# Attention with projections in halves, weighing of two slots in odd ones, and a split of the eight PSUM banks into four, three and one

## What is computed

```python
qh = (q @ Wq + bq).reshape(B, LQ, HEADS, D_K).transpose(0, 2, 1, 3)
kh = (k @ Wk + bk).reshape(B, LKV, HEADS, D_K).transpose(0, 2, 1, 3)
vh = (v @ Wv + bv).reshape(B, LKV, HEADS, D_K).transpose(0, 2, 1, 3)
scores = jnp.einsum('bhqd,bhkd->bhqk', qh, kh) * scale
attn = jax.nn.softmax(scores, axis=-1)
out = jnp.einsum('bhqk,bhkd->bhqd', attn, vh)
```

## Time and profile before

| | us |
|---|---|
| median of 3 runs | 1433.04 |
| lowest, highest | 1431.14, 1434.31 |
| the profiled execution, its own time | 1427.45 |
| its span, first to last instruction | 1425.7 |
| slots 0 to 510 within it | 65.87 to 959.19 |

### The profile page before, as it was taken

One profiled execution on the slowest core, in us unless ns is written; L12 is line 12 of the kernel. 1 busy time (PEld: TensorE's weight loads), 2 busy tenths in 40 slices (PEclk: granted clock), 3 DMA queues, 4 the chain that ended last, 5 costly groups with the idle time before them and its releaser, 6 DMA issues.

```text
span 1425.7 us, 32607 instructions
## 1 busy us (share of the span) xinstructions
PE 1372.8 (96%) x13186; PEld 757.5 (53%) x13186; DVE 1070.9 (75%) x2114; ACT 962.1 (67%) x1931; POOL 287.7 (20%) x321
## 2 busy tenths in 40 slices
PE   7799999999999999999999999998989999989998
PEld 4344444444444444444444545456547999856666
DVE  4787877778787778777778888835876768767757
ACT  5377777777777777777777666672896664448731
POOL 3353121222212222121222100000003100001210
PEclk9899999999999999999999999999999999999999
DMA  5865453335445335544424632002401320347000
GB/s 172 191 160 151 119 134 93 90 92 135 115 122 121 73 90 128 131 113 106 112 68 102 192 83 46 2 1 60 119 24 59 111 68 0 92 117 151 2 1 30
DMA packets 98790, 134.53 MB, mean 94 GB/s; under 512 B 11024, under 2 KB 74128, under 8 KB 92688
## 3 DMA queue, kind: packets, MB, share of 16 engines
q1 hardware_dynamic: 98640, 132.45, 36.8%
HBM read 94.15 MB, written 38.27 MB: 93 GB/s over the span
## 4 chain that ended last, share of the span: by engine, by line
PE 83%; DVE 7%; ACT 7%; issue 2%; DMA 1%; POOL 0%; SPq 0%; DVEq 0%; ACTq 0%; POOLq 0%
PE psum L546 19%; PE psum L566 18%; PE psum L527 7%; PE psum L592 4%; PE psum L632 4%; PE psum L2147 4%; PE psum L2121 3%; PE psum L1241 2%; PE psum L2866 2%; DVE peaks L693 1%; ACT probs L791 1%; ACT key_f L824 1%; PE psum L2876 1%; PE psum L275 1%; PE psum L1638 1%
## 5 line engine op out<-in xcount | busy, mean ns | idle before, releaser
L693 DVE TENSOR_REDUCE peaks<-psum 128x1 f32<-128x512 f32 x1024 | 654.6, 685 | 168.7 <-PE psum L527 157.1
L791 ACT ACTIVATE probs<-psum 128x512 f32<-128x512 f32 x1024 | 555.9, 595 | 126.8 <-PE psum L546 125.0
L546 PE MATMUL psum<-queriesT,keysT 64*128 64x256 bf16 (+1 forms) x4096 | 331.9, 272 | 11.0 <-ACT probs L791 9.8
L566 PE MATMUL psum<-probs,values 128*17 128x256 f32 x4096 | 320.5, 385 | 0.0
L546 PEld LDWEIGHTS psum<-queriesT,keysT 64*128 64x128 bf16 (+1 forms) x4096 | 171.9, 94 | 219.4 <-ACT probs L791 159.3
L527 PE MATMUL psum<-keysT,queriesT 64*128 64x512 bf16 x1024 | 210.2, 379 | 7.3 <-DVE peaks L693 4.0
L566 PEld LDWEIGHTS psum<-probs,values 128*17 128x17 f32 x4096 | 68.0, 95 | 160.4 <-issue 151.3
L927 POOL CAST key_parts<-key_f 128x512 bf16<-128x512 f32 x57 | 34.9, 612 | 516.0 <-ACT key_f L824 509.7
L592 PE MATMUL psum<-ctxT,wk 128*128 128x512 f32 x128 | 75.1, 670 | 2.2 <-DVE probs L736 0.9
L527 PEld LDWEIGHTS psum<-keysT,queriesT 64*128 64x128 bf16 x1024 | 59.8, 94 | 26.1 <-DVE peaks L693 17.5
L632 PE MATMUL psum<-wv,ctxT 128*128 128x256 f32 x256 | 72.0, 407 | 0.5 <-DVE probs L724 0.4
(11 more groups left out here) (315 smaller groups left out, 1647.7 us busy)
## 6 DMA issues: line engine op xcount, KB each, us to landing
keysT<-key_parts SPq DMA_DIRECT2D x186, 256.0 KB, 5.5
key_parts<-key_parts SPq DMA_DIRECT2D x90, 256.0 KB
ctx_nat<-in_ctx_dram SPq DMA_DIRECT2D x32, 256.0 KB, 3.2
ctx_in<-in_ctx_dram SPq DMA_DIRECT2D x24, 256.0 KB, 3.1
ctx_turned<-ctxT SPq DMA_DIRECT2D x24, 256.0 KB, 6.0
ctx_T<-ctx_turned SPq DMA_DIRECT2D x12, 512.0 KB, 3.9
qk_parts<-early_weights SPq DMA_DIRECT2D x24, 128.0 KB
q_parts<-q_parts SPq DMA_DIRECT2D x20, 128.0 KB
```

What stands on the lines that cost most here:

```text
L546: made = e.matmul(ps[j][:, e2 * S:(e2 + 1) * S], self.keysT[own, plane, i % RING, kt * P:(kt + 1) * P], self.queriesT[own, plane, u % 2, g ...
L566: made = e.matmul(k.bank(SUMS)[32 * quad:32 * quad + DH + 1, 0:S], self.values[b % 2][:, kt, g * GH + j, :], self.probs[:, (SLOTS * i + p) ...
L693: e.tensor_reduce(self.peaks[:, i % 2, j * QT + qt, c:c + 1], k.ps(("max", n)), AX.X, ALU.max).then_inc(*self.peaked.up(n))
L791: e.activation(self.probs[:, t % RINGP, 2 * j * S:(2 * j + 2) * S], k.ps(("scores", t, j)), ACT.Exp).then_inc(*self.exped.up((t, j)))
```

## The change

Four things are changed together, in the first attention alone.

- **Banks**: scores rotate through four banks (0, 1, 2, 4) in place of three; maxima and jobs rotate through three (5, 6, 7) in place of four, from slot -1 on.
- **Weighing**: BLOCK is 2 in place of 1. Odd slots weigh the slots t - 3 and t - 2 together, with 16 matmuls in a row; even slots weigh nothing.
- **Halves**: the chunks of keys from the third unit on (u >= 2) are made as two jobs "fill half" of 256 rows, two slots apart. Of the values, the pieces 10 to 15 of a sequence are made as two jobs "make half" of 128 rows. Each half takes a bank and an evacuation of its own. GpSimd splits a chunk after its second half.
- **Slots of the jobs**: those that were in odd slots or shared an even one move, so that the even slots of a sequence carry about one job each (a few carry "turn shift" or "normalize" as well); "write parts" is one slot later.

```diff
-SCORES, SUMS, BLOCK = (0, 1, 2), 3, 1
+SCORES, SUMS, BLOCK = (0, 1, 2, 4), 3, 2
...
+    HALF_VALUES = {10: (-36, -28), 11: (-20, -14), 12: (-12, -6), 13: (-4, 2), 14: (4, 10), 15: (12, 14)}
...
-            at(-16 + 5 * c, "fill keys", 1, c)
+            at(-16 + 5 * c + (c in (5, 7)), "fill keys", 1, c)
...
-                at(slot + 2, "fill keys", u, c)
+                at(slot + 2, "fill half", u, c, 0)
+                at(slot + 4, "fill half", u, c, 1)
                 if c % 2:
-                    at(slot + 6, "write parts", u, c // 2)
+                    at(slot + 7, "write parts", u, c // 2)
...
-                at(SLOTS * NG * b + (8 * p - 96 if p < 12 else (-6, 0, 2, 8)[p - 12]), "make values", b, p)
+                slot = SLOTS * NG * b
+                if p in self.HALF_VALUES:
+                    for e2, after in enumerate(self.HALF_VALUES[p]):
+                        at(slot + after, "make half", b, p, e2)
+                else:
+                    at(slot - 94 + 8 * p, "make values", b, p)
...
-            choice = (7, 0, 1, 2) if t < -1 else (4, 5, 6, 7)
+            choice = (7, 0, 1, 2) if t < -1 else (5, 6, 7)
...
-            if (t - 1) % BLOCK == 0 and BLOCK + 1 <= t <= TOTAL + 1:
+            if t % BLOCK == 1 and BLOCK + 1 <= t <= TOTAL + 1:
                 i, p0 = divmod(t - BLOCK - 1, SLOTS)
                 b, g = divmod(i, NG)
                 w.wait_ge(self.exped, (t - 2, 1))
@@ -591,6 +598,20 @@
...
+                elif job == "fill half":
+                    u, c, h = a
+                    b, m = divmod(u, KD)
+                    ps = misc(t, ("keys", u, c, h), (self.key_kept, (u, c) if h else ("half", u, c)))
+                    w.wait_ge(*self.ctx_turned(b, c))
+                    e.matmul(ps[:, 0:S], self.wk[:, 0, m * P:(m + 1) * P], self.ctxT[:, c * BANK + h * S:c * BANK + (h + 1) * S],
+                             start=True, stop=True).then_inc(*self.key_made.up((u, c) if h else ("half", u, c)))
+                elif job == "make half":
+                    b, p, e2 = a
+                    ps = misc(t, ("v", b, p, e2), (self.v_kept, (b, p) if e2 else ("half", b, p)))
+                    w.wait_ge(*self.ctx_turned(b, 2 * p * P // BANK))
+                    kt = 2 * p + e2
+                    e.matmul(ps[:, 0:D], self.ctxT[:, kt * P:(kt + 1) * P], self.wv[:, 0, :], start=True, stop=True).then_inc(
+                        *self.v_made.up((b, p) if e2 else ("half", b, p)))
...
+                elif job == "fill half":
+                    u, c, h = a
+                    w.wait_ge(self.key_made, (u, c) if h else ("half", u, c))
+                    self.wait_key_f(w, (u, c))
+                    e.activation(self.key_f[:, self.turns[u, c] % 2, h * S:(h + 1) * S], k.ps(("keys", u, c, h))[:, 0:S], ACT.Identity,
+                                 bias=self.bk[:, u % KD:u % KD + 1]).then_inc(*self.key_kept.up((u, c) if h else ("half", u, c)))
+                elif job == "make half":
+                    b, p, e2 = a
+                    w.wait_ge(self.v_made, (b, p) if e2 else ("half", b, p))
+                    e.activation(self.values[b % 2][:, 2 * p + e2, :, 0:DH],
+                                 k.ps(("v", b, p, e2))[:, 0:D].rearrange("p (h d) -> p h d", h=H), ACT.Copy).then_inc(
+                        *self.v_kept.up((b, p) if e2 else ("half", b, p)))
...
+                elif job == "fill half" and a[2]:
+                    yield tuple(a[0:2])
...
-                if job == "fill keys" and not (a[0] == 0 and a[1] in self.ON_VECTOR):
-                    u, c = a
+                if job == "fill half" and a[2] or job == "fill keys" and not (a[0] == 0 and a[1] in self.ON_VECTOR):
+                    u, c = a[0:2]
```

## The result

The changed kernel takes 1467.38 us (median of 4 runs, 1464.18 to 1468.04); the kernel before, beside it, 1432.09 (1426.86 to 1434.31). The ratio is 1.0247, with an interval of 1.0215 to 1.0280: slower by about 35 us. The forecast was 1458 with a range of 1446 to 1472.

What follows compares the result with a forecast made beforehand. TensorE's own order of work was taken as the bound. +20 us for three runs of 128 slots, +1 for slots 0 to 31, +5 for 416 to 491, -1 for the last: +25, median 1433.0 to 1458, range 1446 to 1472.

Steps and rivals of the forecast that it cites:

- The deciding term: Three banks for maxima and jobs: odd slot's second maximum waits to 1.75 us, stalling pairs with a half 0.35 to 0.40.
- rival C: Double weighing: the second weighing saves nothing, 1.12 us rather than 1.02 in 255 pairs, +26 on top, 1483; chance 3%.
- rival B: Odd slot's second maximum: the bank loop binds only in part, gain and loss cancel at 1430 to 1436 us; chance 4%.
- Rival A: Odd slot's second maximum: the bank loop doesn't bind, pairs cost 3.18 us, kernel faster at 1391 to 1403; chance 8%.
- Three runs of 128 slots: The three runs from slot 32 on: pair prices summed to 682.5 us against 661.2, or +21.3, taken as +20 for upward roundings.
- first of the two maxima waits to 1.75: Pairs with a half and the shift: TensorE arrives at 1.61 us, waits for the bank until 1.75, pair 3.55.
- Slots 416 to 491: Stretch with the next part's long steps: VectorE's other work meets a shorter rotation, +1.4 to +8 us, taken as +5.
- rival D: VectorE's side work hits the short rotation everywhere, more in slots 416 to 491: +10 to +30 us, 1468 to 1488; chance 7%.
- The ends: Slots 0 to 31: +1 us (0 to +3); last slots, near ScalarE's exponentials as bound: -1 (0 to -2).
- Costs put at nothing: Halves' extra evacuations on ScalarE, GpSimd starting a chunk two slots later, SyncE writing parts one slot later: no cost.

## Why the prediction was right, and where it was off

**The deciding term held.** The loop of 0.41 + 1.29 + 0.05 = 1.75 us was read on the trace of before; 1.76 was measured. Pairs with a half, values and nothing cost 3.52, 3.59 and 2.93, for 3.55, 3.63 and 2.94. The double weighing is 0.99, for 1.02, so rival C is out, and with the full stall rival B. Waits of maxima for reductions are 85.1 us, where 60 to 90 were said. Rival A, the faster kernel, is what the old banks and the half reductions give: pairs with a half at 3.18 and 3.15 for its 3.18, 128 slots at 212.7 and 212.5 for its 211, and 1416 and 1396 us in all. Its price was about right and its condition not met, since rotation by itself doesn't hide a reader. The Trainium skill ("Perfetto Trace Analysis", section "Optimizing Tensor Performance") advises rotation through banks; these runs agree only where the time between two uses of a bank is longer than the reader takes.

**Three runs of 128 slots: +26.8 us, for +20.** I wrote 3.55 for context with "normalize" and it is 3.94, 4 times; 3.7 for "normalize" with a half and it is 4.0, 3 times; and 4.0 for the three jobs, which take 4.6. The step that failed is "first of the two maxima waits to 1.75": it followed the banks of the maxima and not that of the second job. The turned context is the second use after the even slot's first maximum and "normalize" the third, so that it comes to this maximum's bank. The timeline at such a slot of the kernel after:

```profile
134.54 0.38 PE L534 MATMUL psum<-keysT,queriesT 64*128 64x512 bf16 x2
134.85 0.42 PEld L590 LDWEIGHTS psum<-const,ctx_in 128*128 128x128 f32 x4 [0.32 <-DVE peaks L714]
...
135.70 0.52 PEld L674 LDWEIGHTS psum<-const,outT 128*128 128x128 f32 x4 [0.43 <-DVE peaks L714]
```

By its price it would be there at 0.31 + 0.59 = 0.90 and gets it at 1.16 (134.54 to 135.70), which is my own 0.41 + 0.68 + 0.05 = 1.14 for an empty pair. These eight pairs are worth 3.1 us in 128 slots, 9 in three runs. The other pairs came out up to 0.05 cheaper than I said and give back some 4, so that 21.3 before rounding became 26.8. The roundings did go upwards; that I took 20 for it moved the sum the wrong way all the same.

**Slots 416 to 491: +11 us, for +5, beyond my bound of 8.** Here rival D holds. The timeline at slot 443, where the next part's statistics (L1358 to L1362) run on VectorE:

```profile
869.36 0.69 DVE L1435 TENSOR_TENSOR x<-psum,x 128x512 f32<-128x512 f32 x1 [1.60 <-PE psum L1276]
...
871.29 0.17 DVE L1362 TENSOR_SCALAR small<-small 128x2 f32<-128x2 f32 x1
871.37 2.48 DVE L714 TENSOR_REDUCE peaks<-psum 128x1 f32<-128x512 f32 x4
...
872.10 0.09 PEld L534 LDWEIGHTS psum<-keysT,queriesT 64*128 64x128 bf16 x1 [1.75 <-DVE peaks L714]
872.11 0.39 PE L534 MATMUL psum<-keysT,queriesT 64*128 64x512 bf16 x1 [1.36 <-DVE peaks L714]
```

and the same place in the kernel before:

```profile
837.29 0.69 DVE L1400 TENSOR_TENSOR x<-psum,x 128x512 f32<-128x512 f32 x1 [1.23 <-PE psum L1241]
...
839.30 2.48 DVE L693 TENSOR_REDUCE peaks<-psum 128x1 f32<-128x512 f32 x4
...
840.63 0.09 PEld L527 LDWEIGHTS psum<-keysT,queriesT 64*128 64x128 bf16 x1 [0.32 <-DVE peaks L693]
```

Behind the same burst of 2.0 us the weight load waits 1.75 us in one (TensorE itself is idle for 1.36 of them) and 0.32 in the other. One bank fewer lets VectorE fall behind by less before TensorE stands. Over the whole stretch, maxima wait 18.4 us for reductions, where they waited 3.6. The runs agree: this stretch takes 145.5 and 141.6 us in two kernels with old banks, and 153.1 and 148.0 in their sisters with new ones; without pairs it is 142.1 and 146.1; and with new banks and half reductions it is 139.4. Part of the 11 may be the granted clock, 0.99 here: the kernel with whole jobs, whose work in this stretch is the same, takes 151.6 at 1.00. Outside this stretch D didn't happen: pairs of one kind in 128 slots scatter by 0.01 us.

**The ends.** Slots 0 to 31: +3.0 for +1, at the end of the bound. Maxima wait 7.2 us for reductions there, where they waited 0.4. The granted clock was 0.97 for 1.00, but the kernel with half reductions takes 57.4 us for this stretch's 61.5 at 0.97 too, so the clock isn't the cause. The last slots: -3.3 for -1. The gain is that of the fourth score bank: pairs alone make these slots longer (33.7 for 31.5), the new banks alone shorten them (29.6), and both together give 28.2. I had taken ScalarE's exponentials for their bound, and ScalarE is busy for 21.8 of 28.2 us. Work behind slot 510: +3.6, not touched by the change, and it goes with the granted clock. In the eleven profiled executions this part takes 464.0 to 466.5 us in five, at a mean clock of 0.99 to 1.00, the kernel before among them, and 469.9 to 470.6 in six, at 0.97, the kernel after among them.

**Costs put at nothing.** Evacuations of halves (478 ns each for 687 of a whole) and the later transfers make TensorE wait nowhere in the kernel after. The half-reduction kernel has them all. There maxima wait for the evacuation of a half 21 times, by 0.2 us at most and 3.4 in all, and its pairs still have their bare price.

All in all +37.4 us up to slot 510 for +25, with the sign, the mechanism and the place right, and the sum short by a third. That is beyond my bounds of +19 to +31 for it, even with the 3 to 4 for roundings. The total, 1467.4 for 1458, lies in the range of 1446 to 1472 by some luck: the range had been stretched to 1472 for rival D, and the medians lie 35.3 us apart where the two profiled executions lie 40.6 apart, since the one before is 4.6 us under the median of 1432.1 and the one after 0.7 over its own.

## What to carry to other kernels

When a change shortens what lies between two uses of a buffer, write down for every use, jobs too, how long ago its bank was taken, and compare that with the reader's latency (here 0.41 us to start, 0.65 for each reduction, 0.05 to hand over), however idle the reader is on average. Do it for every pool that shares the banks: with seven to share, the one moved to scores took 0.16 us off an empty pair (3.09 to 2.93) and put 0.34 on a pair with a half (3.18 to 3.52). Ask next whether the change has to be made everywhere: weighing in pairs only where a job already stands between the scores gave 31 us with no new bank at all.

## What the runs showed of the hardware

- A change of matmul form on TensorE (bfloat16 with 64 rows to float32 with 128 and back) costs about 0.09 us each way: maxima take 0.31 us ahead of a float32 group and 0.22 ahead of scores. The double weighing fits with it: 0.99 us for two in a row, 0.56 for one, so two in a row cost 0.13 less than two apart. The Trainium skill ("Perfetto Trace Analysis", section "Optimizing Tensor Performance") says that larger matmuls are more efficient than smaller ones; here a job of half the columns takes 0.63 for 1.06 us, so two cost 0.20 more than one.
- Two matmuls of 64 rows can run side by side: the two maxima of a slot take 0.38 us together, at 379 ns each. Held apart by a wait they take 0.75, so the group's busy time went from 210.2 us to 259.2 on the same work, while TensorE's share stayed at 96%. The idle time of weight loads tells it, 17.5 against 85.1 us.
- Two reductions of 256 columns take 0.76 us and two of 512 take 1.29, so half the columns cost 59%.
- In 20 executions of one and the same kernel before, the mean granted clock lay between 0.983 and 0.994 and the time between 1425.8 and 1435.5 us. In one long part that no edit touches, behind slot 510, the eleven traces fall in two groups: 464.0 to 466.5 us at a mean granted clock of 0.99 to 1.00, and 469.9 to 470.6 at 0.97. So two executions can differ by 3 to 7 us in this part alone, along with the clock.
